# Fetching a second stage's weights in small pieces during attention, instead of in one burst

## The reference

```
g     = einsum('oc,bct->bto', Wg, x) + bg            # Wg, Wtheta, Wphi: 32 x 64
theta = einsum('oc,bct->bot', Wtheta, x) + btheta
phi   = einsum('oc,bct->bot', Wphi, ctx) + bphi
f     = softmax(einsum('bci,bcj->bij', phi, theta))  # 256 x 256 for each batch entry
w_y   = einsum('oc,btc->bot', Wz, f @ g) + bz
x     = gamma*(w_y - mean)*rsqrt(var + 1e-5) + beta + x   # mean, var over batch and time
```

## Time and profile before

| what | value |
|---|---|
| median of three runs | 730.25 us (729.62 to 730.59) |
| profiled execution, its own time | 732.31 us |
| its span, first to last instruction | 730.5 us |
| mean granted TensorE clock | 0.965 |
| busy: TensorE, VectorE, ScalarE, GpSimd | 635.5, 637.0, 362.0, 262.1 us |
| bytes moved by DMA | 54.18 MB, of which GpSimd's queue (software_dynamic) 3.43 MB |
| GpSimd's longest pause | 124.9 us, between the chain on the weights and `norm_params` |

### The profile page before, as it was taken

How to read it: one execution, slowest core, us unless ns; L and a number is a source line. 1 busy time by engine, 2 the same in 40 slices (tenths; PEclk the granted TensorE clock), 3 DMA queues, 4 the chain that set the end, 5 groups by cost and what they waited for, 6 DMA issues and landing times.

```text
span 730.5 us, 9667 instructions
## 1 busy us (share of the span) xinstructions
PE 635.5 (87%) x2704; PEld 351.7 (48%) x2704; DVE 637.0 (87%) x1001; ACT 362.0 (50%) x799; POOL 262.1 (36%) x189
## 2 busy tenths in 40 slices
PE   7789999997996778999889899989988989995796
PEld 5466666665542223444435445344443534533365
DVE  2489999995467999999999999999999999979954
ACT  3468888882233317245444644625554472451343
POOL 1850000000002765636337355453733536452000
PEclk9689999999998997999999999999999999998799
DMA  2711222220066056053432705515161360560000
GB/s 64 217 45 57 57 59 63 64 59 3 28 132 127 1 115 144 1 115 79 95 64 51 172 0 115 131 41 114 55 119 40 75 144 0 115 133 12 0 30 29
DMA packets 38332, 54.18 MB, mean 74 GB/s; under 512 B 4643, under 2 KB 21187, under 8 KB 38179
## 3 DMA queue, kind: packets, MB, share of 16 engines
q1 hardware_dynamic: 36882, 50.46, 31.1%
q0 software_dynamic: 1424, 3.43, 1.5%
HBM read 16.13 MB, written 4.19 MB: 28 GB/s over the span
## 4 chain that ended last, share of the span: by engine, by line
DVE 31%; PE 18%; issue 16%; POOL 4%; ACT 3%; DMA 2%; SPq 1%; DVEq 1%; ACTq 0%; POOLq 0%
DVE state L1423 13%; PE ps_a L794 4%; PE ps_a L823 3%; DVE x L1386 3%; PE ps_c L880 2%; DMA vb<-v 2%; POOL state L685 2%; DVE state L1410 2%; PE ps_a L806 2%; DVE st L1354 2%; POOL x L690 1%; DVE sx L1520 1%; SPq L630 1%; DVE sx L1501 1%; PE ps_att L860 1%
## 5 line engine op out<-in xcount | busy, mean ns | idle before, releaser
L690 POOL TENSOR_TENSOR x<-x,xn 128x1024 f32<-128x1024 f32 x35 | 87.5, 2502 | 199.2 <-DVE x L1386 199.2
L1423 DVE TENSOR_TENSOR_SCAN state<-ps_w,state 128x512 f32<-128x512 f32 x128 | 145.8, 1200 | 0.7
L794 PE MATMUL ps_a<-x,wsq 128*128 128x512 f32 x256 | 118.2, 602 | 5.9 <-ACT xn L1124 3.0
L685 POOL TENSOR_TENSOR state<-vb,k 128x2016 f32<-128x2016 f32 x23 | 107.3, 4664 | 23.7 <-DMA vb<-v 15.6
L1428 DVE TENSOR_TENSOR vb<-state,r 128x2048 f32<-128x2048 f32 x32 | 96.6, 3018 | 1.7
L794 PEld LDWEIGHTS ps_a<-x,wsq 128*128 128x128 f32 x256 | 47.5, 192 | 65.9 <-issue 52.3
L823 PE MATMUL ps_a<-mix_t,w 128*128 128x512 f32 x128 | 62.5, 610 | 15.6 <-DVE x L1386 9.6
L1386 DVE SCALAR_TENSOR_TENSOR x<-ps_a,vec,sx 128x512 f32<-128x512 f32 x80 | 57.2, 744 | 13.3 <-PE ps_a L823 12.0
L296 ACT ACTIVATE probs<-ps_f,negmax 128x256 f32<-128x256 f32 x128 | 59.1, 473 | 2.0 <-DVE negmax L345 1.2
L345 DVE TENSOR_REDUCE negmax<-ps_f 128x2 f32<-128x512 f32 x64 | 41.2, 686 | 7.9 <-PE ps_f L218 5.5
L823 PEld LDWEIGHTS ps_a<-mix_t,w 128*128 128x128 f32 x128 | 22.5, 189 | 50.8 <-DVE x L1386 17.3
(11 more groups left out here) (203 smaller groups left out, 1233.7 us busy)
## 6 DMA issues: line engine op xcount, KB each, us to landing
vb<-v SPq DMA_DIRECT2D x128, 256.0 KB, 5.8
x<-in_x SPq DMA_DIRECT2D x32, 128.0 KB, 2.1
c<-in_ctx SPq DMA_DIRECT2D x32, 128.0 KB, 2.1
x_chunk<-in_x SPq DMA_DIRECT2D x8, 512.0 KB, 7.4
out<-sx SPq DMA_DIRECT2D x7, 512.0 KB, 3.5
wsq<-in_wsq POOLq DMA_DIRECT2D x1, 1024.0 KB, 5.4
wsq<-in_wsq POOLq DMA_DIRECT2D x1, 768.0 KB, 6.9
s<-in_s POOLq DMA_DIRECT2D x1, 512.0 KB, 7.9
```

What stands on the lines that cost most here:

```text
L685: nc.gpsimd.tensor_tensor(st[q][:, :, :, 1:L], src[:, :, :, 0:L - 1], wide(k[p][h][:, :])[:, :, :, 0:L - 1], ALU.mult).then_inc(kv_at(n, h ...
L690: nc.gpsimd.tensor_tensor(x5[j % 2][:, :, :], x5[j % 2][:, :, :], xn[:, :, 1:L1], ALU.add).then_inc(x5_ready, 1)
L794: mm = nc.tensor.matmul(bank[:, :], wsq[:, weight, c, P * o:P * o + P], src(c), start=(c == 0), stop=(c == EC - 1))
L1423: nc.vector.tensor_tensor_scan(row, w[h][:, :], row, 0.0, ALU.mult, ALU.add).then_inc(scanned, 1)
```

## The change

The burst of GpSimd is cut into single steps. A helper `after_pair(pi)` makes GpSimd wait until pair pi (counted from 0) has landed. The two DMAs that fetched seven square matrices (1024 and 768 KB) become seven of 256 KB, and the state's 512 KB become two of 256 KB, so there are 38 DMAs and `LATE` is 38. The first three pieces wait for pair 3 as before, each further one for a pair of its own, up to pair 16; the six low-rank pieces wait for pair 17; the sixteen reordering ones go out four at a time with pairs 18 to 21. Beside this the last two stores get a semaphore of their own, for which SyncE waits at the end, and a function on GpSimd is defined at another place in the file.

```diff
-LATE = 32
+LATE = 38
@@ attention, GpSimd
-            pool.wait_ge(s_xin[1], 64)
-
-            for dst, src in ((t["cst"][:, ONES:ID, :], d["cst"][:, C_ONES:C_ID, :]), (t["vec"], d["vec"]), (t["bnv"], d["bnv"]), (t["wsq"][:, 0:WO], d["wsq"][:, 0:WO]), (t["wsq"][:, FK:], d["wsq"][:, FK:]), (t["w1"][:, :, 0:5 * MIX], d["w1"]),
-                             (t["dw1"], d["dw1"]), (t["s0"], d["s0"]),
-                             (t["prev1"], d["prev1"]), (t["prev0"], d["prev0"])):
+
+            def after_pair(pi):
+                pool.wait_ge(s_xin[pi % 2], 32 * (pi // 2 + 1))
+
+            for i, (dst, src) in enumerate(((t["cst"][:, ONES:ID, :], d["cst"][:, C_ONES:C_ID, :]), (t["vec"], d["vec"]), (t["bnv"], d["bnv"]), *((t["wsq"][:, w], d["wsq"][:, w]) for w in range(8) if w != WO),
+                             (t["w1"][:, :, 0:5 * MIX], d["w1"]),
+                             (t["dw1"], d["dw1"]), *((t["s0"][:, h], d["s0"][:, h]) for h in range(2)),
+                             (t["prev1"], d["prev1"]), (t["prev0"], d["prev0"]))):
+                after_pair(max(3, i + 1))
                 pool.dma_start(dst[(slice(None),) * len(dst.shape)], src).then_inc(t["s_late"], 16)
             pool.wait_ge(s_pad, 3)
+            after_pair(17)
             for i in range(4):
...
             for e in range(S):
                 rows = slice(HH * e, HH * e + HH)
+                after_pair(18 + e // 2)
@@ rwkv, SyncE
-                sp.dma_start(out[lo:lo + 2].rearrange("a p f -> p a f"), y_last[:, 2 * i:2 * i + 2, :]).then_inc(stored, 16)
+                sp.dma_start(out[lo:lo + 2].rearrange("a p f -> p a f"), y_last[:, 2 * i:2 * i + 2, :]).then_inc(last_stored, 16)
...
-            sp.wait_ge(stored, 16 * CHUNKS + 32)
+            sp.wait_ge(stored, 16 * CHUNKS)
+            sp.wait_ge(last_stored, 32)
```

More of the change, by code:

```diff
@@ L487, in rwkv @@
     last_xk, last_xr, last_key, last_relu, last_kk = sem("last_xk_ready"), sem("last_xr_ready"), sem("last_keys_done"), sem("last_relu_ready"), sem("last_kk_ready")
-    last_rec, last_rr_ready, last_val, last_y, last_ready = sem("last_recept_done"), sem("last_rr_ready"), sem("last_values_done"), sem("last_y_mid"), sem("last_out_ready")
+    last_rec, last_rr_ready, last_val, last_y, last_ready, last_stored = sem("last_recept_done"), sem("last_rr_ready"), sem("last_values_done"), sem("last_y_mid"), sem("last_out_ready"), sem("last_stored")
     v_spread = [sem("v_spread_0"), sem("v_spread_1")]
@@ L686, in b_kv @@
                                         ALU.mult).then_inc(kv_at(n, h, q)[0], 1)
-            def add_x(n, j):
-                pool.wait_ge(mod_ready, n * 10 + 2 * j + 2)
-                nc.gpsimd.tensor_tensor(x5[j % 2][:, :, :], x5[j % 2][:, :, :], xn[:, :, 1:L1], ALU.add).then_inc(x5_ready, 1)
             def last_rstd2(i):
@@ L697, in last_rstd2, with add_x @@
                 nc.gpsimd.tensor_tensor(rs2[:, 1, cut], ve2[:, 1, cut], rs2[:, 0, cut], ALU.mult).then_inc(last_ln, 1)
+            def add_x(n, j):
+                pool.wait_ge(mod_ready, n * 10 + 2 * j + 2)
+                nc.gpsimd.tensor_tensor(x5[j % 2][:, :, :], x5[j % 2][:, :, :], xn[:, :, 1:L1], ALU.add).then_inc(x5_ready, 1)
             def fill_pass(n, p):
```

## The result

| | median | runs | ratio to the kernel before |
|---|---|---|---|
| before, beside it | 730.16 us | 4 | |
| with the change | 724.75 us (722.73 to 725.07) | 4 | 0.992 (95% interval 0.9901 to 0.994) |
| with the change, once more | 723.77 us (722.61 to 724.87) | 6 | 0.9918 (0.989 to 0.9947), against 729.5 us |

The change makes the kernel 5.4 to 5.7 us faster. 721.6 us was forecast, a gain of 8.7, with a range of 719.2 to 726.5. The profiled execution of the changed kernel took 722.73 us (span 720.9), 9.6 us less than the profiled one of before; so the two profiles differ by more than forecast, the medians by less. Part of this was found: executions of one and the same kernel differ by several us, also in parts that the change doesn't touch.

A forecast was written before the change was run, and what follows sets the result against it. GpSimd's burst was taken to delay a context tile, stall TensorE and lower its clock in the early attention stage. Gains of 6.31 + 2.37 = 8.68 us, other terms 0, took the 730.25 us median to 721.6; range 719.2 to 726.5.

The forecast's parts named there:

- The hole: Early attention stage: TensorE's projection waits 5.40 us for a context tile delayed by GpSimd's burst; removing this gains 6.31 us.
- The slow body: Pair 3's body, right behind the hole, at the lower clock: 4.46 instead of 6.83 us, a gain of 2.37 us.
- The chain: GpSimd's preparation of late weights, moved to about 104 to 116 us: price stays 1.90 us, so nothing gained or lost.
- Issues and waits on GpSimd: Attention stage: 38 DMA issues instead of 32 cost 0, at most 1.9 us; added waits have 48 us of room.
- Pieces beside tiles: Attention stage: each 256 KB piece takes 0.8 us beside the next pair's tiles, against 1.7 us of slack; cost 0.
- the signs: Attention stage, if right: tiles land under 3.8 us, full clock from about 24 us, second stage 8 to 9 us earlier.
- B: Rival: GpSimd's preparation chain costs more in undisturbed attention bodies, 5 us, giving 724.7 us; chance 0.10.
- C: Rival: TensorE's clock stays or falls low after the early bodies, costing 4.7 us, so 726.3 us; chance 0.08.
- D: Rival: the early context tile wasn't late by the burst, so nothing is gained, 730.2 us; chance 0.03.
- E: Rival: the pieces make every pair's tiles late in 16 attention bodies, 7.3 us slower, 737.6 us; chance 0.05.
- the forecast's own: Range of whole time without rivals: 719.7 us (chain costs nothing) to 723.5 us (issues cost 1.9); forecast's chance 0.74.

The follow-up runs named there:

- warm3: The changed kernel with three throwaway TensorE matmuls in its pause of 1.6 us ahead of the scores of pair 1: 721.15 us, ratio 0.986.
- after_warm: The changed kernel with six throwaway TensorE matmuls ahead of the scores of pair 1: 720.2 us, ratio 0.9868.

## Why the prediction was right, and where its size was off

**The hole.** Right. It was the tile of 21.84 us behind the burst, and it moved with the burst. It was priced from one execution at 6.31 us, and between the two first profiles just this was gained (a body of 10.77 us became one of 4.46). But it has no fixed size: another execution shows 4.85, and the moved burst a body 5.48 us over the usual.

**The slow body.** The mechanism was right: 6.83 and 6.87 us in two profiles, directly behind the hole. The size is the step that failed. 2.37 us was taken as a fixed loss; in the second profile of before it was 0.30, in the one with the moved burst 2.41. Hole and slow body together were 8.68 us in the profile that was read and 5.15 in the other. The prediction had the warning in hand: the profiled execution lay 2.06 us over the median. It took that surplus for an offset common to both kernels. Had it been taken for part of the losses that the change removes, the gain would have been 8.68 - 2.06 = 6.6 us and the time 723.6 us, within 1.2 us of both medians. This is a fit after the fact: against its second profile the first had 3.5 us more in hole and slow body and 1.6 more in body 1, but 1.2 less in the chain's bodies and 2.1 less behind the stage. Which of these the timed executions had is not on record.

**The chain.** Right, and close: 2.31 and 2.20 us in the two profiles of the changed kernel, against the 1.90 carried over. What the prediction didn't see is that the clock can be down in such a body as well (0.77 on average in the long one of warm3, 1.00 in that of the changed kernel's first profile): 3.08 us in the second profile of before, 3.49 with large pieces, 3.06 with the squares at once, 3.11 in warm3, 4.7 behind the moved burst. The rule of the Trainium skill ("SBUF — State Buffer", section "SBUF: two separate sides") that the shared ports are held for a whole instruction is borne out by the cut: the held scaling fell from 2.51 to 0.82 us once the instruction was in eight. The prediction's sentence that this price "cannot be saved by moving the chain within this stage" left out that most of it can be saved by cutting the instruction.

**Issues and waits on GpSimd.** Taken as 0. Until the chain begins all bodies take 4.46 us and all scaling pairs about 0.62, beside 38 issues. The chain began at 102.6 us, forecast 104.5, and left 48 us of room.

**Pieces beside tiles.** Taken as 0, and it was 0. One landing of 4.1 us, over the 3.8 that the signs allowed, made a projection wait 0.37 us, but no body longer. The piece beside it had 256 KB, issued at 37.42 us, 1.6 us ahead of the tile, which at the 319 GB/s of the earlier trace rows explains 0.8 us. Why this tile took 4.1 us is open; the wait comes in the body of pair 6 in five of the nine profiles with pieces of 256 KB one at a time (0.17 to 0.45 us).

**The rivals.** B, the chain at 5 us: not in the changed kernel's two profiles, but 3.5 us were seen with large pieces and 4.7 behind the moved burst. C, the clock low in early bodies: it didn't fall again behind 22 us before the chain. But body 1, ahead of the point that the prediction looked at, was longer by 1.1 to 2.8 us in some executions of both kernels; the clock was back for body 2 each time. D: refuted by the moved burst. The rule of the Trainium skill beside it ("DMA: Bandwidth & Descriptors", section "Queues, rings and completion order", turns packet by packet) can't be read here as equal turns in bytes: 1.75 MB in pieces of 256 KB held a tile back to 5.8 us, and they need 5.5 us at 319 GB/s. E: refuted; the changed kernel's slowest landings were 4.1 and 3.3 us, and no body grew by them.

**The range and the signs.** The median of 724.75 us lies in the range of 719.2 to 726.5 and outside the forecast's own of 719.7 to 723.5. Of the signs, the full clock from about 24 us and the unchanged rest of the program came. The second stage began 9.8 us earlier instead of 8 to 9, and pairs 3 and 6 were early, both by luck in body 1. That a profile gained 9.6 us is therefore no confirmation of the forecast's 8.7.

## What to carry to other kernels

Before a loss that one profile shows is booked as a gain, compare that execution with the median: a surplus may be part of the loss itself, and two profiles of one kernel can differ in where they lose. Weights for a later stage can be fetched while an earlier one runs if no more is queued at a time than the running stage's own loads have slack for; here the amount queued counted, not the size of a piece. A long GpSimd instruction beside VectorE's work that TensorE waits for cost nearly its own length (2.0 of 2.39 us), and cutting it in eight gave 1.4 us of that back.

## What the runs showed that was not expected

- One kernel's executions on one chip spread over 9.0 us (723.73 to 732.72). Three causes are seen in the profiles: whether TensorE's granted clock falls in or behind pauses of 1.6 us (body 1 took 4.5, 5.6 or 7.2 us for the same work), whether it is low at the start of the norm parameters (1.3 to 1.7 us), and a race between VectorE and GpSimd in the last chunk, within 0.33 us, that decides over 4.2 us. How they share in the spread of the timed executions, which have no trace, is not shown.
- A time can fall far from the edit: in its one profile after_warm had a first stage 0.2 us shorter than the changed kernel's and a span 4.3 us shorter, and nearly all of it lay in the last chunk's race.
- A projection that waited 0.33 to 0.37 us for its tile made no body longer; a wait of 2.11 us cost 1.7.
